# A transformer layer with two cross attentions on one core: TensorE's transposes of the identity matrix left out of the filling and emptying rounds

## What is computed

```python
ln_out = layernorm(hidden_states, ln1_s, ln1_b)
q, k, v = jnp.split(ln_out @ w_qkv + b_qkv, 3, axis=-1)
x = hidden_states + merge_heads(attention(q, k, v, ltor_mask)) @ w_ao + b_ao
q = layernorm(x, ln2_s, ln2_b) @ w_q + b_q
k, v = jnp.split(encoder_states @ w_kv + b_kv, 2, axis=-1)
x = x + merge_heads(attention(q, k, v, cross_mask)) @ w_co + b_co
x = x + gelu(layernorm(x, ln3_s, ln3_b) @ w1 + b1) @ w2 + b2
# second module
a = _layer_norm(audio_kv, ln_gamma, ln_beta)
out = attention(x @ Wq.T, a @ Wk.T, a @ Wv.T) @ Wo.T
return x + jnp.tanh(gate) * out
```

## Time and profile before

| | before |
|---|---|
| median of 3 runs | 888.63 us |
| the runs | 887.2, 888.63, 890.95 us |
| the profiled execution | 887.42 us |
| its span, first to last instruction | 885.6 us |
| mean granted clock of TensorE | 0.990 |
| PE busy | 850.9 us, 96% |
| VectorE, ScalarE, GpSimd busy | 75%, 65%, 63% |

### The profile page before, as it was taken

One profiled execution on the slowest core, in us unless ns is written; L12 is line 12 of the kernel. 1 busy time (PEld: TensorE's weight loads), 2 busy tenths in 40 slices (PEclk: granted clock), 3 DMA queues, 4 the chain that ended last, 5 costly groups with the idle time before them and its releaser, 6 DMA issues.

```text
span 885.6 us, 24680 instructions
## 1 busy us (share of the span) xinstructions
PE 850.9 (96%) x9940; PEld 813.2 (92%) x9940; DVE 660.4 (75%) x1474; ACT 573.8 (65%) x1083; POOL 557.4 (63%) x565
## 2 busy tenths in 40 slices
PE   7878999999999999999999999999999999999996
PEld 7877889999999999999999999999999999998885
DVE  5868758778787777877777778778787787778454
ACT  5544858577584848758484866758485775848443
POOL 1456756749294765929486683938567492956351
PEclk9889999999999999999999999999999999999999
DMA  9010100100101010110101010010101001010000
GB/s 298 7 31 15 45 1 14 46 13 9 49 3 45 14 45 13 32 28 2 44 14 45 13 46 14 2 46 13 45 13 46 14 7 39 2 45 2 27 13 13
DMA packets 34143, 26.76 MB, mean 30 GB/s; under 512 B 12784, under 2 KB 33392, under 8 KB 34032
## 3 DMA queue, kind: packets, MB, share of 16 engines
q1 hardware_dynamic: 34032, 25.20, 9.8%
HBM read 20.99 MB, written 4.19 MB: 28 GB/s over the span
## 4 chain that ended last, share of the span: by engine, by line
POOL 44%; PE 34%; DVE 10%; issue 6%; ACT 4%; DMA 0%; POOLq 0%; SPq 0%; DVEq 0%; ACTq 0%
POOL prob_AC L1897 11%; POOL prob_B L1891 8%; POOL h_lo L1904 8%; POOL prob_AC L1891 8%; POOL prob_B L1897 5%; PE s_bank L566 5%; PE s_bank L541 4%; PE pj L439 3%; PE pj L492 3%; POOL rstd L1877 3%; PE pj L500 2%; PE pj L494 2%; PE pj L470 2%; PE pj L478 2%; PE pj L472 2%
## 5 line engine op out<-in xcount | busy, mean ns | idle before, releaser
L1877 POOL TENSOR_TENSOR rstd<-var_eps,half 128x2 f32<-128x2 f32 x64 | 45.5, 711 | 200.3 <-DVE var_eps L1402 200.3
L1897 POOL TENSOR_TENSOR prob_AC<-prob_AC,rmax_C 128x512 f32<-128x512 f32 x64 | 68.5, 1072 | 82.8 <-DVE rmax_C L1356 82.7
L1008 ACT ACTIVATE prob_AC<-s_bank 128x512 f32<-128x512 f32 x128 | 73.7, 616 | 70.7 <-PE s_bank L552 70.5
L1000 ACT ACTIVATE k<-pj,kbias,consts 128x256 f32<-128x256 f32 x192 | 92.7, 566 | 31.2 <-PE pj L478 26.6
L541 PE MATMUL s_bank<-k,q 64*128 64x128 f32 x1536 | 102.0, 282 | 6.3 <-ACT q L987 4.4
L541 PEld LDWEIGHTS s_bank<-k,q 64*128 64x128 f32 x1536 | 91.9, 190 | 13.6 <-ACT q L987 4.8
L1891 POOL TENSOR_TENSOR prob_AC<-prob_AC,maskA_off 128x512 f32<-128x512 f32 x64 | 81.5, 1286 | 15.0 <-DVE prob_AC L1351 15.0
L1891 POOL TENSOR_TENSOR prob_B<-prob_B,maskB_off 128x512 f32<-128x512 f32 x64 | 82.2, 1295 | 6.8 <-DVE prob_B L1351 6.5
L960 ACT ACTIVATE oT_AC_hi<-pj,bias 128x256 fp32r<-128x256 f32 x64 | 26.9, 472 | 88.3 <-PE pj L579 88.3
L1904 POOL TENSOR_TENSOR h_lo<-g,h_hi 128x512 fp32r<-128x512 f32 x64 | 82.4, 1296 | 1.2 <-DVE h_hi L1862 1.2
L552 PE MATMUL s_bank<-consts,prob_AC 128*128 128x128 f32 x512 | 72.9, 275 | 9.0 <-POOL prob_AC L1897 7.8
(11 more groups left out here) (209 smaller groups left out, 2690.5 us busy)
## 6 DMA issues: line engine op xcount, KB each, us to landing
x_in<-in_x SPq DMA_DIRECT2D x16, 256.0 KB, 2.8
ctx_b<-in_ctx_features SPq DMA_DIRECT2D x16, 256.0 KB, 3.0
ctx_c<-in_ctx SPq DMA_DIRECT2D x16, 256.0 KB, 3.0
out<-y SPq DMA_DIRECT2D x16, 256.0 KB, 2.2
maskB<-in_mask_Bx1xSxS_ff SPq DMA_DIRECT2D x32, 64.0 KB, 2.7
g<-in_w_M SPq DMA_DIRECT2D x2, 512.0 KB, 6.5
prob_AC<-in_w_A_qkv SPq DMA_DIRECT2D x3, 256.0 KB, 4.2
prob_B<-in_w_B_kv SPq DMA_DIRECT2D x2, 256.0 KB, 4.2
```

Of the source, the lines that this page charges most:

```text
L1000: last = nc.scalar.activation(k2[:, m, :, s, :], k_all[:, m], ACT.Identity, bias=kbias[:, "ABC".index(a), s, m:m + 1], scale=parity[:, 2 + ...
L1008: nc.scalar.activation(prob[a][:, r, :, :].rearrange("p n k -> p (n k)"), s_bank[r][:, :], ACT.Exp).then_inc(turned_in[a], 1)
L1877: nc.gpsimd.tensor_tensor(rstd[:, n, :], var_eps[:, n, :], half[:, :], ALU.pow).then_inc(ln_rstd[l], 1)
L1897: nc.gpsimd.tensor_tensor(p3, p3, rmax[a][:, r, :].unsqueeze(2).broadcast_to([P, BL * TILE, S]), ALU.subtract).then_inc(shifted[a], 1)
```

## The change

All 33 calls of `keep_busy` go: 6 in round 0, 13 in round 1, 3 in round 2, 1 in round 3, 1 in round U+1, 2 in round U+2 and 7 in round U+3. With four transposes each, that is 132 instructions of PE. The function stays and is not called. Nothing else is changed, and the other engines run the same instructions in the same order.

```diff
             def fill0(i):
-                keep_busy("P.cA", i + 1)
...
+                pass
...
             def fill1(i):
                 carry_shifts("A", i, 0, 3)
                 pe.wait_ge(ln_done["A"], unit("A", i) + 1)
                 turn("A.zT", z["A"], i)
-                keep_busy("A.K", i)
-                keep_busy("A.K", i)
                 carry_shifts("A", 1, 1, 3)
                 carry_shifts("A", 1, 2, 3)
-                keep_busy("A.K", i)
                 feature_major("A.K", i)
...
                 scores("A", 0, i)
-                keep_busy("P.cM", i)
                 scores("A", 1, i)
-                keep_busy("P.cM", i)
-                keep_busy("P.cM", i)
                 carry_shifts("M", i, 0, 4)
-                keep_busy("A.OT", i)
-                keep_busy("A.OT", i)
                 carry_shifts("M", 1, 1, 4)
                 turn_probs("A", 0, i)
-                keep_busy("A.OT", i)
                 turn_probs("A", 1, i)
                 values("A", 0, i)
-                keep_busy("A.OT", i)
-                keep_busy("A.OT", i)
                 turn_probs("A", 2, i)
                 turn_probs("A", 3, i)
                 values("A", 1, i)
-                keep_busy("A.OT", i)
                 carry_shifts("M", 1, 2, 4)
                 turn_out("A", i)
-                keep_busy("A.AO", i)
                 token_major("A.AO", i)
...
-                keep_busy("B.Q", i)
                 feature_major("B.Q", i)
...
                 turn_out("B", i)
-                keep_busy("B.AO", i)
                 turn_probs("A", 2, i)
...
-                keep_busy("A.AO", i)
                 token_major("A.AO", i)
...
-                keep_busy("B.OT", i)
                 values("B", 1, i)
...
                 turn_probs("B", 1, i)
-                keep_busy("C.AO", i)
                 turn_probs("B", 2, i)
...
                 turn_probs("C", 3, i)
-                keep_busy("M.Y0", i)
-                keep_busy("M.Y0", i)
                 values("C", 0, i)
...
                 feature_major("C.Q", i)
-                keep_busy("C.OT", i)
                 scores("C", 0, i)
-                keep_busy("C.OT", i)
                 scores("C", 1, i)
-                keep_busy("C.OT", i)
-                keep_busy("C.OT", i)
                 turn_probs("C", 0, i)
                 turn_probs("C", 1, i)
-                keep_busy("C.OT", i)
                 turn_probs("C", 2, i)
                 turn_probs("C", 3, i)
                 values("C", 0, i)
                 values("C", 1, i)
-                keep_busy("C.OT", i)
                 turn_out("C", i)
-                keep_busy("C.AO", i)
                 token_major("C.AO", i)
```

## The result

| | before | after |
|---|---|---|
| first timing, median of 6 and 6 runs | 888.66 us | 895.35 us |
| ratio, 95% interval | | 1.0082 [1.0059, 1.0104] |
| second timing, on one chip, median of 35 and 12 runs | 888.88 us | 893.33 us |
| ratio, 95% interval | | 1.0055 [1.0033, 1.0077] |
| profiled execution, its span | 887.42, 885.6 | 895.71, 893.9 |

A forecast was written before the change was run, and what follows sets the result against it. PE's own work, 96% busy, was taken to pace the full rounds. Terms summing to +5.3 us on the profiled 887.42 gave 892.7; forecast 893.3, between this and 893.9 from the median; range 889.0 to 897.8.

The forecast's parts named there:

- What bounds the kernel: Full rounds: PE, busy 96% of the span, sets the pace; the clock can matter only in the rounds at both ends.
- The transposes raise and hold the clock: Start and later waits: identity transposes alone bring PE from 212 to 110 ns each, so removing them loses clock.
- The rival that they hold nothing: Whole kernel: only the transposes' own time on the chain goes, -2.4 us, to 885.0 or 886.2; chance 0.08.
- Start: 1.4 us, ends 0.8 and 2.9: Rounds 0 and 1: shift products and first projections run at 1.2 GHz, so A.V ends 1.4 us late.
- Round 1, second half, +0.1 and 0.4: Low clock from before 33 us: turn and values cost more, four transposes go, +0.1; output projection's clock returns later, 0.4.
- Rounds 2, 3 and U+1: 0: Groups there stand in front of waits for other engines, so removing them changes next to nothing, 0 us.
- Round U+2: -0.45: Value products near 851 us start earlier once 8 transposes go, -0.45 us; ScalarE's exponentials become the limit.
- The risk that it carries: Round U+2: the thinner stretch may let the clock fall, slowing PE's dense work behind it, up to +1.7 us.
- Last round: +3.85: Clock low from before the fourth turn at 875.50; turn, values, output transposes and projection slow, +3.85 us, ends 0 and 4.8.
- The sum: Whole kernel: 1.4 + 0.1 + 0.4 - 0.45 + 3.85 = +5.3 us, with all of the start's loss reaching the end.
- The line between slower and no change: Whole kernel: 893.1 us, about 0.5% (4.4 us) from no change; slower by more had chance 0.51, within 0.46.

The follow-up runs named there:

- the one with their time filled otherwise: Kernel before, each last-round group of four identity transposes replaced by two one-column products of the identity; 890.44 against 888.88 us, ratio 1.0033.
- one without the middle's groups: Kernel before without the 10 groups of round 1 from the scores on (40 transposes); 888.34 against 888.61 us, ratio 1.0001.
- one with eight more: Kernel before with 8 more groups (32 identity transposes) in PE's wait between the two score products of round 2; 890.63 against 888.88 us, ratio 1.0031.
- the start's alone: Kernel before without the 24 transposes of round 0 and the 12 of round 1 ahead of A.K; 888.55 against 888.61 us, ratio 0.9993.

## Why the prediction was right, point by point

**What bounds the kernel.** Right in that the change is worth nothing there: at the transposed output of round 2 and at the scores of round U+2 the changed kernel is late by 4.6 and 5.0 us, so the full rounds pass a delay on, and the 0.3 between is less than the 2.15 us by which they differ from one execution to another. That PE's own work sets their pace was read from its busy share alone. The chain in the page of before goes through GpSimd for more of the span than through PE, and no run tests which of the two it is:

```profile
POOL 44%; PE 34%; DVE 10%; issue 6%; ACT 4%; DMA 0%; POOLq 0%; SPq 0%; DVEq 0%; ACTq 0%
```

**The transposes raise and hold the clock.** Right in the last round: with the groups the clock holds in eight profiles of eight, without them it falls in three of three, and in the one with their time filled otherwise. The rival that they hold nothing (885 to 886) is out by both timings.

**Start: 1.4 us, ends 0.8 and 2.9.** Right against the profile, 1.0 and 1.5 at its two landmarks. One reading in it is off: A.V's end before was put at 21.1, which has the run-out of the last record in it, while the 22.4 is where the next group can start. That was 20.91 before, so the same working gives 1.5; 22.44 came. Wrong as a property of the kernel: over 12 runs it is nothing that can be measured. The step that failed is that I priced the state of one profile, in which the 24 transposes' clock lasted until z_A came; in two of the six profiles it did not, and then the groups behind z_A cost their own low price.

**Round 1, second half, +0.1 and 0.4.** Profile 0.3 and 0.7. The low clock from before 33 us was from 27.4. Right in kind, a little small: the 32 value records took 1.92 and not 2.05, and the four transposes gave back 0.91 and not 1.05, from start to start, but the shift products behind them took 0.16 more, which was not in the sum.

**Rounds 2, 3 and U+1: 0.** The step that was mis-sized: 2.2 us in the profile. The groups there were rightly priced, but I took the fall at 60.2 as something that the change does not touch. In the changed kernel the clock fell at 65.0 and once more at 71.8, and stayed down over turns and value products that had run at full speed. It is no fixed cost: the second profile of the same kernel does not have it, nor has the one without any group of rounds 0 to 3, and two have it, one without the middle's groups and one with eight more. None of the five profiles whose groups from the scores of round 1 to the end of round 2 are those of before has it. Whether the change makes it more frequent stays open.

**Round U+2: -0.45.** 0.40 in the profile, and the limit is where it was said to be: the four exponentials run from 854.46 to 856.53, two of them are done at 855.5, and the values start at 855.64. The risk that it carries (a fall just behind it) was seen in one of three profiles, at 1.5 us.

**Last round: +3.85.** 3.75 in the profile, and 3.8 in the second profile; 2.6 to 3.5 in the median of the run without its groups alone, whose own profile has 0.65, since the clock comes back early in the values. How often it does so is not shown. The largest term, and right in size and place. Two of its parts were off against each other: the 64 value records took 1.57 more and not 1.85, and what is behind them 1.72 more and not 1.58.

**The sum.** 5.3 against 4.45 and 6.7 in the two pairs of medians and 8.3 between the profiles. Counting from halfway between the profiled run and the median gave 893.3, and the two medians are 893.3 and 895.35. The mechanism of the largest term is right; that one median meets the forecast to the tenth is luck. The sum holds 1.4 us of the start that no median shows and nothing for round 2 or for a fall in round U+2, each of which one of the two profiles has. The line between slower and no change ran through the forecast; both timings, 1.0055 and 1.0082, lie on its slower side, and the interval of one reaches across it.

## To carry to other kernels

Work that exists only to keep TensorE awake is worth asking for at the places where PE is the single thread behind a wait: here the last round, whose 28 transposes are worth 3.8 us in two profiles, 0.65 in a third and 2.6 to 3.5 in the median, while the 92 in the filling rounds are worth 2.6 together and the start's alone nothing that can be measured. Replace such work one place at a time, and judge it by a dozen runs and their granted clock, not by one profile: a single profile of this kernel has the clock's falls at places that the next execution moves. Where profiles are at hand, compare the same stretch in all of them: that settled the last round here, where medians of 12 runs did not. And look at the clock, not at PE's busy share, to see whether such work does its job: in the profile with one-column products PE was as busy and lost the clock.

## What the runs showed of the hardware

- Four float32 transposes of 128 by 128 and four records of one-column float32 products take PE the same time: 8 one-column records 0.95 us and 1.84 at the two levels of the clock, 4 transposes 0.44 from start to start at the high one. With the transposes the clock stayed at 1.00 through the last round in eight profiles of eight; with the products it fell at 876 in the one profile.
- The Trainium skill, page "TensorE: Matmul & The Clock Gate", Part 4: PE-mode transpose, has it that the full rate doesn't engage for transposes. The traces here do not agree for float32 transposes of 128 by 128 (their records do not say which mode they run in): the clock rose after transposes alone, from 212 to 110 ns each, and with 28 of them the last round's clock stayed up.
- The clock record opens at 1.00 in all twelve profiles, though the first records run at the low price. In the changed kernel it reads 1.00 over the first 20 us, while the shift products take 213 ns each. Until the first edge the durations of like records show the level.
- The spread of this kernel's times, 7.4 us, goes with the place of the clock's edges: with 0.994 and more granted it takes 885.8 us, with 0.986 890.5. Some of it arises at full clock: the same full rounds took 759.05 to 761.20 us.
